# Twelve-layer mixed transformer on one core: layernorms closed in two parts, a router taken tile by tile, and more filler matmuls in a second expert layer

## What is computed

```
for L in 0..3:
    x = x + xattn_L(layernorm(x), ctx_768)
    x = x + attn_L(layernorm(x))
    x = x + ffn_L(layernorm(x))
```

## Time and profile before

| | |
|---|---|
| median of 3 runs | 1504.36 us |
| the profiled execution | 1496.21 us |
| its span, first to last instruction | 1494.4 us |
| mean granted TensorE clock in it | 0.944 |
| PE busy | 1349.1 us (90%) |
| DVE busy | 924.5 us (62%) |
| ACT busy | 604.4 us (40%) |
| POOL busy | 53.3 us (4%) |
| DMA read and written | 143 GB/s over the span |

### The profile page before, as it was taken

How to read it: one execution, slowest core, us unless ns; L and a number is a source line. 1 busy time by engine, 2 the same in 40 slices (tenths; PEclk the granted TensorE clock), 3 DMA queues, 4 the chain that set the end, 5 groups by cost and what they waited for, 6 DMA issues and landing times.

```text
span 1494.4 us, 22399 instructions
## 1 busy us (share of the span) xinstructions
PE 1349.1 (90%) x9052; PEld 896.3 (60%) x9052; DVE 924.5 (62%) x1683; ACT 604.4 (40%) x868; POOL 53.3 (4%) x67
## 2 busy tenths in 40 slices
PE   4988789899999999989898999999999898896987
PEld 2456468445556655777683556556556577783543
DVE  4545531488888888355415888888883467624434
ACT  4612111166666666223103666666651235431302
POOL 0000000100000000000001000000000012310000
PEclk9996999999999999999759999999999879997998
DMA  5310116157666677720220667766677126650000
GB/s 191 123 57 1 57 57 253 57 174 211 208 213 205 203 219 227 256 82 2 88 85 25 210 191 224 220 215 191 221 224 270 42 98 239 231 193 0 1 0 15
DMA packets 106070, 215.84 MB, mean 144 GB/s; under 512 B 10864, under 2 KB 76528, under 8 KB 98544
## 3 DMA queue, kind: packets, MB, share of 16 engines
q1 hardware_dynamic: 104816, 206.03, 42.5%
q0 software_dynamic: 1152, 8.39, 1.5%
HBM read 146.74 MB, written 67.63 MB: 143 GB/s over the span
## 4 chain that ended last, share of the span: by engine, by line
PE 63%; DVE 19%; DMA 8%; issue 4%; ACT 2%; POOL 2%; SPq 1%; POOLq 0%; DVEq 0%; ACTq 0%
PE ps L237 24%; PE ps L1824 3%; PE ps L1837 3%; PE ps L1825 3%; PE ps L1804 3%; PE ps L1826 3%; PE ps L1838 3%; PE ps L1805 2%; PE ps L1807 2%; PE ps L1806 2%; DMA blocks<-wk 2%; DMA xn_both<-blocks 2%; PE ps L1768 2%; DMA ring<-blocks 2%; PE ps L1810 2%
## 5 line engine op out<-in xcount | busy, mean ns | idle before, releaser
L613 ACT ACTIVATE wk<-ps,wk 128x1024 f32<-128x1024 f32 x128 | 142.7, 1115 | 196.3 <-DVE wk L1030 196.2
L1030 DVE TENSOR_REDUCE wk<-ps 128x1 f32<-128x1024 f32 x128 | 155.7, 1217 | 92.5 <-PE ps L1810 92.5
L622 ACT ACTIVATE wk<-wk 128x1024 f16<-128x1024 f32 x128 | 184.9, 1445 | 56.1 <-DVE wk L1037 51.9
L1043 DVE SCALAR_TENSOR_TENSOR wk<-wk 128x1024 f16<-128x1024 f32 x128 | 179.1, 1399 | 1.2 <-ACT wk L622 1.2
L237 PE MATMUL ps<-wk,ring 128*128 128x128 f32 (+3 forms) x896 | 148.6, 334 | 10.3 <-DVE wk L1249 2.8
L1048 DVE STREAM_TRANSPOSE wk<-wk 128x1024 f32<-128x1024 f32 x128 | 156.9, 1226 | 0.1
L237 PEld LDWEIGHTS ps<-wk,ring 128*128 128x128 f32 x896 | 130.2, 229 | 25.7 <-issue 12.6
L237 PE MATMUL ps<-ring,wk 128*128 128x256 f32 (+2 forms) x456 | 102.9, 378 | 4.2 <-DVE wk L1355 1.6
L1804 PE MATMUL ps<-ctx_T,ring 128*128 128x512 f16 x256 | 97.2, 380 | 3.6 <-DVE ring L1026 3.0
L1807 PE MATMUL ps<-ctx_T,ring 128*128 128x512 f16 x256 | 96.9, 379 | 0.0
L1806 PE MATMUL ps<-ctx_T,ring 128*128 128x512 f16 x256 | 96.9, 379 | 0.0
(11 more groups left out here) (346 smaller groups left out, 2177.1 us busy)
## 6 DMA issues: line engine op xcount, KB each, us to landing
blocks<-wk SPq DMA_DIRECT2D x512, 128.0 KB, 3.6
ring<-blocks SPq DMA_DIRECT2D x40, 1024.0 KB, 5.5
ring<-units SPq DMA_DIRECT2D x34, 1024.0 KB, 6.4
xn_both<-blocks SPq DMA_DIRECT2D x22, 1024.0 KB, 5.6
ring<-experts SPq DMA_DIRECT2D x16, 1024.0 KB, 6.7
ring<-context SPq DMA_DIRECT2D x16, 384.0 KB, 4.2
wk<-context SPq DMA_DIRECT2D x16, 384.0 KB, 3.3
wk<-blocks SPq DMA_DIRECT2D x2, 1024.0 KB, 4.7
```

Source lines behind the costliest of these rows:

```text
L613: ACTE.activation(blocks, bank(2 * (t % 2), 2, 4, 128), ACT.Exp, bias=WNM[:, t % 4:t % 4 + 1], accum_out=WRS[:, t % 4:t % 4 + 1]).then_inc ...
L622: ACTE.activation(weight_halves(t)[0], WXP[:, t % 2, :], ACT.Identity, scale=WRI[:, t % 4:t % 4 + 1]).then_inc(xa_PH, 1)
L1030: DVE.tensor_reduce(WNM[:, t % 4:t % 4 + 1], bank(2 * (t % 2), 1024), X, ALU.max, negate=True).then_inc(xa_max, 1)
L1043: DVE.scalar_tensor_tensor(low, WXP[:, t % 2, :], WRI[:, t % 4:t % 4 + 1], high, ALU.mult, ALU.subtract).then_inc(xa_PL, 1)
```

## The change

- Every layernorm is closed in two parts. The statistics of tiles 0 to 2 are closed (a helper `close`) as soon as tile 2's are taken, before tile 3 is added; tile 3 follows alone. POOL raises 3 columns, then 1, with a signal each. DVE waits for the first ahead of tile 0 and for the second ahead of tile 3.
- The transposes of tiles 0 and 1 go to bank 0 and those of tiles 2 and 3 to bank 1, with a signal for each pair; ACT copies tiles 0 and 1, DVE tiles 2 and 3. With gain and bias each side has two instructions instead of one.
- Layer 8's output is added tile by tile, after the first pair of tiles and the second, and the statistics are taken with each. Layer 9's own layernorm takes its statistics tile by tile as the tiles are normalised.
- Layer 2's router has an RDL buffer for each tile. DVE builds the first, ACT the other three in 24 instructions of 128x64. TensorE spreads all four, then gathers each tile when its SEL is there, with `keep_clock(5)` ahead of each. DVE makes SEL tile by tile after the counts; SELG for all four after that. ACT copies XIN of tiles 0 to 2 and SGTH after them, DVE copies XIN of tile 3. The 44 and the 8 filler matmuls go, and the wait for SGTH and SGTL moves from ahead of `up(0)` to ahead of `down(0)`.
- Layer 5: `keep_clock(16)` becomes `keep_clock(20)`, and `keep_clock(10)` is added between the gather and the wait for L1f_comb.

The diff, cut to its core (waits on renumbered semaphores of layer 8 left out):

```
     def rsqrt(n):
-        pool.wait_ge(ln_stats, n + 1)
-        r = rstd[:, 0:NT]
-        POOL.tensor_tensor(r, r, C("nhalf")[:, 0:NT], ALU.pow).then_inc(ln_rstd, 1)
+        for part, tiles in enumerate((slice(0, 3), slice(3, 4))):
+            pool.wait_ge(ln_stats, 2 * n + part + 1)
+            r = rstd[:, tiles]
+            POOL.tensor_tensor(r, r, C("nhalf")[:, tiles], ALU.pow).then_inc(ln_rstd, 1)
...
     # ACT, layernorm
-        act.wait_ge(ln_T, LNT[key] + 1)
+        act.wait_ge(ln_T, 2 * LNT[key] + 1)
+        turned = bank(0, 2, 2, 128)
+        first = xnT[:, :, 0:256].rearrange("p c (i t) -> p c i t", t=128)
-            ACTE.copy(xnT[:, 0, :], ps[:, 0, :]).then_inc(ln_xnT, 1)
+            ACTE.copy(first, turned.rearrange("p i c t -> p c i t")).then_inc(ln_xnT, 1)
...
     # ACT, router of layer 2
+    act.wait_ge(rk_diag, 1)
+    for i in range(1, NT):
+        for e in range(8):
+            ins = ACTE.activation(RDL[i][:, e, :], C("delta"), ACT.Identity, scale=RP[:, i, e:e + 1])
+        ins.then_inc(rk_diag_act, 1)
+    for i in range(3):
+        act.wait_ge(gathered, i + 1)
+        ACTE.copy(XIN[:, :, :, i, :], bank(i, 2, 8, 32)).then_inc(xin_copied, 1)
     act.wait_ge(comb_T, 1)
     ACTE.copy(SGTH, bank(6, 8, 128)).then_inc(comb_Ts, 1)
-    for i in range(0, NT, 2):
-        act.wait_ge(gathered, i + 1)
-        ACTE.copy(XIN[:, :, :, i, :], bank(i, 2, 8, 32)).then_inc(xin_copied, 1)
...
     # DVE
+    def close(tiles):
+        for i in tiles:
+            ins = DVE.bn_aggr(mv[:, i, :], st6[:, i, :])
+        link(ins)
+        tiles = slice(tiles[0], tiles[-1] + 1)
+        DVE.tensor_scalar(rstd[:, tiles], mv[:, tiles, 1], 1e-5, None, ALU.add).then_inc(ln_stats, 1)
+    def stats(i, src=x):
+        ins = DVE.bn_stats(st6[:, i, :], src[:, i, :])
+        if i >= 2:
+            link(ins)
+        if i == 2:
+            close((0, 1, 2))
...
-        dve.wait_ge(ln_rstd, n + 1)
+        close((3,))
         for i in range(NT):
+            if i == 0 or i == 3:
+                dve.wait_ge(ln_rstd, 2 * n + (2 if i else 1))
             DVE.tensor_scalar(xn[:, i, :], src[:, i, :], mv[:, i, 0:1], rstd[:, i:i + 1], ...)
...
     def places(i):
         dve.wait_ge(rk_spread, i + 1)
         # as ranks before, for one tile
         link(DVE.tensor_reduce(RK[:, i, :], RG, X, ALU.add))
+        DVE.tensor_tensor(SEL[:, i], ..., ALU.is_equal).then_inc(L0f_sel, 1)
+    for i in range(NT):
+        places(i)
+    dve.wait_ge(L0f_sel, 4)
...
     # TensorE, layernorm
-            ins = PE.transpose(ps[:, c, 128 * i:128 * i + 128], xn[:, i, 128 * c:128 * c + 128], ident)
-    ins.then_inc(ln_T, 1)
+            ins = PE.transpose(bank(i // 2, 128, at=256 * (i % 2) + 128 * c), xn[...], ident)
+        if i % 2:
+            ins.then_inc(ln_T, 1)
...
     # TensorE, layer 2
-    spread_scores(0)
-    keep_clock(44, 7)
-    pe.wait_ge(L0f_sel, 1)
     for i in range(NT):
+        spread_scores(i)
+    for i in range(NT):
+        keep_clock(5, 7)
+        pe.wait_ge(L0f_sel, i + 1)
         for c in range(2):
             ins = mm(bank(i, 256, at=256 * c), xn[:, i, 128 * c:128 * c + 128], SEL[:, i])
         ins.then_inc(gathered, 1)
+    pe.wait_ge(L0f_sel, 5)
     for e in range(8):
         ins = PE.transpose(bank(6, 128, at=128 * e), SELG[:, e], ident)
     ins.then_inc(comb_T, 1)
-    keep_clock(8, 4)
     pe.wait_ge(xin_copied, 4)
-    pe.wait_ge(comb_Ts, 2)
...
         up(e + 1)
+    if e == 0:
+        pe.wait_ge(comb_Ts, 2)
     down(e)
...
     # TensorE, layer 5
-    keep_clock(16, 7)
+    keep_clock(20, 7)
     pe.wait_ge(L1f_disp, 1)
     # gather, as before
+    keep_clock(10, 7)
     pe.wait_ge(L1f_comb, 1)
```

More of the change, by code:

```diff
@@ L305, in build @@
         RS1 = wv(9788, 8)
-        RDL = wv(7232, 8, 64)
+        RDL = [wv(7232 + 512 * i, 8, 64) for i in range(NT)]
         RG, RE, RBEF = wh(5184, 8, 64), wh(5696, 8, 64), wh(6208, 64)
@@ L1417, in _, with places @@
             link(DVE.tensor_tensor(RP, RP, bc8(RB_), ALU.mult))
-            ranks(0)
-            for i in range(NT):
-                ins = DVE.tensor_tensor(SEL[:, i], RK[:, i, :].unsqueeze(2).to_broadcast([128, 8, 32]),
-                                        C("slot32").unsqueeze(1).to_broadcast([128, 8, 32]), ALU.is_equal)
-            chain[0] += 1
-            ins.then_inc(dve_step, 1)
-            dve.wait_ge(dve_step, chain[0])
+            DVE.tensor_tensor(RDL[0], RP[:, 0, :].unsqueeze(2).to_broadcast([128, 8, 64]),
+                              C("delta").unsqueeze(1).to_broadcast([128, 8, 64]), ALU.mult).then_inc(rk_diag, 1)
+            DVE.tensor_copy(RBEF, C("before"))
+            def places(i):
+                dve.wait_ge(rk_spread, i + 1)
+                other = bank(2 + i, 8, 64)
+                mine = RP[:, i, :].unsqueeze(2).to_broadcast([128, 8, 64])
+                DVE.tensor_tensor(RG, other, mine, ALU.is_gt)
+                link(DVE.tensor_tensor(RE, other, mine, ALU.is_equal))
+                link(DVE.tensor_tensor(RE, RE, RBEF.unsqueeze(1).to_broadcast([128, 8, 64]), ALU.mult))
+                link(DVE.tensor_tensor(RG, RG, RE, ALU.add))
+                link(DVE.tensor_reduce(RK[:, i, :], RG, X, ALU.add))
+                DVE.tensor_tensor(SEL[:, i], RK[:, i, :].unsqueeze(2).to_broadcast([128, 8, 32]),
+                                  C("slot32").unsqueeze(1).to_broadcast([128, 8, 32]), ALU.is_equal).then_inc(L0f_sel, 1)
+            for i in range(NT):
+                places(i)
+            dve.wait_ge(L0f_sel, 4)
             for i in range(NT):
@@ L1429, in _ @@
             ins.then_inc(L0f_sel, 1)
-            for i in range(1, NT, 2):
-                dve.wait_ge(gathered, i + 1)
-                DVE.tensor_copy(XIN[:, :, :, i, :], bank(i, 2, 8, 32)).then_inc(xin_copied, 1)
+            dve.wait_ge(gathered, 4)
+            DVE.tensor_copy(XIN[:, :, :, 3, :], bank(3, 2, 8, 32)).then_inc(xin_copied, 1)
             dve.wait_ge(comb_Ts, 1)
@@ L1446, in _ @@
                 link(ins)
[L1447 to L1449 removed]
+                stats(i)
             layernorm(3)
@@ L2266, in self1, with spread_scores @@
                 project_out(l, (4, 5, 6, 7), lambda c, i: SO[:, c, tile(i)], lambda c: wo[:, c, :], 2, used=1)
-            def spread_scores(k):
-                for i in range(NT):
-                    pe.wait_ge(rk_diag, 4 * k + i + 1)
-                    mm(bank(2 + i, 512), C("same"), RDL).then_inc(rk_spread, 1)
+            def spread_scores(i):
+                pe.wait_ge(rk_diag_act if i else rk_diag, i if i else 1)
+                mm(bank(2 + i, 512), C("same"), RDL[i]).then_inc(rk_spread, 1)
             layernorm(0, n=0)
```

71 lines of the change are left out of this document (25 added, 46 removed).

## The result

| | before | after |
|---|---|---|
| median of the runs | 1505.97 us (4 runs, 1504.28 to 1508.18) | 1446.38 us (4 runs, 1438.36 to 1453.19) |
| profiled execution | 1496.21 us | 1449.55 us |
| its span | 1494.4 us | 1447.7 us |
| mean granted clock in it | 0.944 | 0.958 |

The ratio is 0.9601, 95% interval 0.9545 to 0.9658: some 60 us faster, where the prediction said 35, and outside its range (1457 to 1488). The direction was right and the size was not.

What follows compares the result with a forecast made beforehand. It took engines working one after the other to bound the touched places, TensorE leading the last chain with 63%. Layernorms 8.9, router 11.5 and second expert layer 14.7 sum to 35.1; 1504.4 less that gives 1469 us, range 1457 to 1488.

Steps and rivals of the forecast that it cites:

- Layernorms, 8.9: All layernorms: closing tiles 0 to 2 early shortens the chain, 8.9 us in sum, between 3 and 11.
- upper bound: Common layernorms: tile 3 ends at 104.15 instead of 104.84, at most 0.69 us each; 0.6 was taken.
- the rival of a second power that blocks DVE: Layernorms: POOL's power costs a fixed 1.01 us and nine layernorms gain nothing; 1476 us, chance 0.10.
- First router, 11.5: Layer 2's router: counting starts after one spread, gathers run behind each tile; 11.5 us, between 8 and 13.
- Second expert layer, 14.7: Layer 5: fillers keep full clock for two groups of 64 records, the third falls partway; 14.7 us, 0 to 21.7.
- The rival in which the thin stream loses the clock by itself: Layer 5: the clock falls within the first microseconds of the stream; 1484 us, chance 0.21.
- 777.61 to 781.29: Layer 5 trace before: nothing but transposes ran and full clock followed, held against the rule that transposes count differently.
- TensorE's filler only covers waiting: Layernorm 1: the work is one chain, and TensorE's filler matmuls only cover waiting; no size given.
- the 8.2 us: Whole kernel: the median lies 8.2 us above the profiled execution, a difference carried over into the forecast.
- The slower rival: Second self attention, 645 to 704: it falls to half clock and layer 5 is not held; 1512 us, chance 0.03.

Runs made afterwards that it cites:

- the router's trace: Kernel before with only layer 2's router changed, also called the router alone: 1485.28 us, ratio 0.9863.
- the fillers alone: Kernel before with only layer 5's two filler counts changed (16 to 20, and 10 new ones): 1489.59 us, ratio 0.9897.
- the filled gap: Changed kernel with 4 more filler matmuls in layer 5's idle 0.90 us ahead of the third group of 64 records: 1451.08 us, ratio 0.9650.
- the whole: The complete change against the kernel before, run again in the same rounds as its separate parts: 1447.92 us, ratio 0.9620.
- the layernorm part: Kernel before with only the layernorms changed, router and fillers as before: 1476.09 us, ratio 0.9819.
- layernorms and router: Changed kernel without layer 5's new fillers: 1457.61 us, ratio 0.9677.
- after with 4 fillers: Changed kernel with 4 instead of 8 filler matmuls in each common layernorm: 1452.34 us, ratio to before 0.9657.
- the further gaps filled: Changed kernel with layer 5's 0.90 us gap filled, plus fillers in layer 9's own layernorm and layer 8's router: 1448.31 us, ratio 0.9633.
- the second idle time filled: Changed kernel with 3 more fillers in each common layernorm, between its transposes and the wait for the copies: 1454.88 us, ratio 0.9632.
- the second trace with 4 fillers in layernorm 5: Kernel before with only the layernorms changed, and layernorm 5's fillers cut from 8 to 4, traced a second time: 1481.67 us, ratio 0.9842.

## Why the prediction was right and wrong

**Layernorms, 8.9.** Close to the rest (10.0), but in part by luck, since the rows give 13.7. The nine common ones bring 9.4 instead of 5.4, 0.97 each and 1.3 in layernorms 3 and 6, all above the "upper bound" of 0.69: the closing of three tiles delays tile 3's addition by 0.43 and not 0.58, and DVE normalises 1.20 after that addition begins and not 1.29. Layernorms 10, 9 and 0 bring 1.4, 1.5 and 1.4 where 1.1, 1.4 and 1.0 were said. The powers took 0.86 and 0.65 against 0.85 and 0.53, and the rival of a second power that blocks DVE is dead: 1.38 for the four normalisings with POOL's 0.65 inside them. By the Trainium skill (SBUF — State Buffer, "SBUF: two separate sides") a DVE instruction that needs the port pair it shares with GpSimd waits for the whole of a GpSimd instruction that started first. No such time is there beside the power of 0.65, while POOL's additions of 256 columns still stretch a normalising (2.20 for four before; one of 0.82 in the kernel after).

**First router, 11.5.** Its layer is 97.6 us long in the router's trace against 110.3, with 3 us less at half clock: 11.2 after taking half of that off. ACT's 24 activations took 5.84 and nobody on DVE waited for them. Counting starts 2.9 after the first spread where 3.5 was said, and takes 3.3 a tile where 3.4 was said. What was not in it are some 2 us in the rest and 6.5 of clock.

**Second expert layer, 14.7.** Right in size and mechanism for the fillers alone: 12.4 in their own trace (77.5 to 65.1 us for the layer), 13.7 in the trace after, the third group falling after 2.3 us of it where 1.5 was said, and the filled gap shows that the 0.90 lets the clock fall. In the whole the term is not the fillers' own, since the layernorm part without them already brings the layer to 58.0 to 60.9. The rival in which the thin stream loses the clock by itself falls: in all 14 traces that entered it at full clock the first two groups ran through in 7.3 to 7.4 each. By the Trainium skill (TensorE: Matmul & The Clock Gate, "Part 4: PE-mode transpose") transposes do not count as the engine being busy in the same way. The prediction took 777.61 to 781.29 against it, but no run here isolates anything; the stream held with eight of them at its head.

**What failed is the step that took layer 5, "the largest term", for the only place where the clock could be won, and put half-clock time everywhere else at nothing**, and with it the layernorm terms that counted DVE's chain and called TensorE's side mere cover ("TensorE's filler only covers waiting"). The page of before had the other dips (6, 7 and 7 in the 4th, 33rd and 37th slice), and the prediction gave no reason why they should stay. The sum was 35.1; the whole brought 57.4. The difference of 22.3 is, term by term: 3.9 more in the rest (24.3 against 8.9 + 11.5), which is about what the layernorms' rows have above their term; 0.7 in layer 5 (51 us at half before and 20.5 after, so 15.4 against 14.7); and 17.7 from half-clock time outside layer 5, 138 us a run before (189 - 51) and 102.5 after (123 - 20.5), if layer 5 in all runs is as in the traces. It lies in no one place: from the two traces of before to those of after, layer 1 goes from 27.3 and 34.1 to 23.9 and 23.9 us, layer 2 from 10.6 and 6.8 to 4.1 and 3.4, layer 6 from 6.8 and 13.1 to none and 3.4, layer 8 from 34.2 and 33.1 to 30.8 and 28.2, layer 9 from 10.2 and 21.5 to 10.1 and 9.4, layer 11 from 12.7 and 13.0 to 9.2 and 9.9. Together these traces show 27 us less outside layer 5, where the runs have 35. The idle time that the change takes from a layernorm's TensorE (0.95 us in layernorm 1) was never priced. That the idle time is a cause of it is shown in kind by the kernel before with longer fillers (15 us less at half, 8 us of time), against 41 us less at half with the layernorm part. What brings the other 26 or so stays open.

**The reference execution.** The one that was profiled had 166 us at half clock, where the 11 runs beside the experiments had 170 to 208. The prediction saw the 8.2 us between it and the median, put them down to where the dips fall and carried them over, which was right for the sum and cost it the hint: 161 to 219 us at half clock in the 50 runs of before beside the experiments means that much is decided from one execution to the next, and an edit may move such odds.

**The slower rival** (the second self attention at half clock) did not come in the whole: 645 to 700 stands at 0.94 after, with 6.8 us at half clock in the layer and 3.4 in the second trace. But it is real: the layer had 17 to 27 us at half in six traces of other variants (the router alone, layernorms and router, after with 4 fillers, the further gaps filled, the second idle time filled, and the second trace with 4 fillers in layernorm 5), and was 76.6 to 81.5 us long there, against 71.3 and 74.4 in the two traces of before.

## What to carry to other kernels

Work out the time at half clock from every run's span and clock before you price a change: it was 189 us here, and an edit that shortens TensorE's idle time can move it, whatever the edit is for; 4 more fillers in a layernorm moved it by 15 us. Fill idle gaps just ahead of thin streams in which TensorE is the bound, as the new fillers of layer 5 do; those where another engine is the bound brought nothing here. One trace does not tell where the clock falls: one kernel gave 77.8 and 60.9 us for the same layer in two executions. And check in each trace that an edit to an idle time has changed that idle time; in one of these two it had not.

## What was not expected of the hardware

- An idle time of 0.90 us in a stream whose 64-column records keep TensorE busy was followed by half clock within some 3 us in 9 of 10 traces that reached it at full clock, and in none of the four in which it was filled. In three of those four, half clock came at the next idle time, of 1.38 us, instead.
- Two idle times of 1.61 and 2.18 us ahead of the same stream were followed by no fall in five traces of five, when the clock had been full at the layernorm before; when it had fallen there, it fell again at the stream in six of six. In those six the slower fillers had covered the 1.61, and only the 2.18 stood ahead of the stream.
- POOL's power took 0.86 us for three columns and 0.65 for one beside DVE's `tensor_scalar`, without stretching it.
